# Decoding a codebook layer's weights one stage earlier: comparisons on GpSimd, three of four quarters inside the single-head attention

## The reference

```python
x = x + _L3_xattn_ref(_layernorm(x), ctx_4096, ...)   # cross-attention, 32 heads, 2048 keys
x = x + _L3_attn_ref(_layernorm(x), ...)              # one head of 128
x = x + _L3_ffn_ref(_layernorm(x), codebooks, bias, ln_weight, codes, centroids)

def _L3_ffn_ref(x2, ...):
    cw = _expand(centroids, codebooks)                # 32 x 512, looked up in 32 codebooks of 32 entries x 16
    dots = x2 @ cw.T
    dots = (dots - mean(dots)) * rsqrt(var(dots) + 1e-05) * ln_weight
    m = softmax(dots) > 0.5
    W = _expand(codes, codebooks)                     # 512 x 512, looked up in the same way
    y = x2 @ W.T + bias
    return y * (any(m, row)[:, None] & repeat(any(m, column), 16)[None, :])
```

## Time and profile before

| what | us |
|---|---|
| median of 3 runs | 1691.44 |
| the runs | 1689.5 to 1693.83 |
| the profiled execution | 1685.28 |
| its span, first to last instruction | 1683.5 |
| first TensorE instruction of L3a, of L3f | 1643.92, 1656.44 |
| GpSimd busy, of the span | 324.6 (19%) |
| TensorE busy, of the span | 1562.3 (93%) |

### The profile page before, as it was taken

How to read it: one execution, slowest core, us unless ns; L and a number is a source line. 1 busy time by engine, 2 the same in 40 slices (tenths; PEclk the granted TensorE clock), 3 DMA queues, 4 the chain that set the end, 5 groups by cost and what they waited for, 6 DMA issues and landing times. The chain is left out here.

```text
span 1683.5 us, 23015 instructions
## 1 busy us (share of the span) xinstructions
PE 1562.3 (93%) x7457; PEld 1167.1 (69%) x7457; DVE 1044.1 (62%) x2136; ACT 889.3 (53%) x1624; POOL 324.6 (19%) x280
## 2 busy tenths in 40 slices
PE   4999999999999988998989996997999999999986
PEld 4788778778775443487566664785777787777864
DVE  5666666675665882275478883664157667676663
ACT  4545554554554451264148884552266667666661
POOL 0000000000001340054136663450011011111110
PEclk9999999999999999999999998998999999999999
DMA  7011011011019107262362212536311122211012
GB/s 259 27 38 57 30 37 62 25 58 42 25 54 364 43 24 266 99 194 97 100 153 29 33 20 87 170 122 231 113 61 53 44 81 80 76 56 56 25 58 79
DMA packets 57282, 148.52 MB, mean 88 GB/s; under 512 B 5969, under 2 KB 28113, under 8 KB 48129
## 3 DMA queue, kind: packets, MB, share of 16 engines
q1 hardware_dynamic: 57216, 147.72, 26.8%
HBM read 133.55 MB, written 8.65 MB: 84 GB/s over the span
## 5 line engine op out<-in xcount | busy, mean ns | idle before, releaser
L1288 DVE TENSOR_TENSOR L3x_k_lo<-bank,L3x_k_hi 128x512 fp32r<-128x512 f32 x128 | 86.0, 687 | 52.2 <-ACT L3x_k_hi L1177 51.9
L2488 POOL TENSOR_TENSOR L2x_p_lo<-L2x_e_t,L2x_p_hi 128x512 fp32r<-128x512 f32 x80 | 105.3, 1326 | 63.0 <-ACT L2x_p_hi L2673 62.4
L664 DVE TENSOR_TENSOR L0x_k_lo<-bank,L0x_k_hi 128x512 fp32r<-128x512 f32 x128 | 85.7, 688 | 42.5 <-ACT L0x_k_hi L577 42.1
L376 PE MATMUL bank<-L0x_ctx_hi,L0x_w_hi 128*128 128x512 f32 x256 | 103.7, 405 | 4.2 <-DVE L0x_ctx_lo L603 4.2
L577 ACT ACTIVATE L0x_k_hi<-bank 128x512 fp32r<-128x512 f32 x128 | 74.2, 599 | 54.7 <-PE bank L482 54.7
L378 PE MATMUL bank<-L0x_ctx_hi,L0x_w_lo 128*128 128x512 f32 x256 | 101.0, 395 | 0.0
L886 POOL TENSOR_TENSOR L3x_v_lo<-L3x_v_raw,L3x_v_hi 128x512 fp32r<-128x512 f32 x32 | 40.5, 1302 | 310.2 <-ACT L3x_v_hi L1168 310.2
L377 PE MATMUL bank<-L0x_ctx_lo,L0x_w_hi 128*128 128x512 f32 x256 | 100.2, 391 | 0.0
L2716 DVE CUSTOM_DVE_ANT_0 L2x_junk<-bank,L2x_mask 128x512 f32<-128x512 f32 x128 | 85.1, 688 | 20.2 <-PE bank L2574 10.8
L1177 ACT ACTIVATE L3x_k_hi<-bank 128x512 fp32r<-128x512 f32 x128 | 74.1, 604 | 41.6 <-PE bank L1046 41.2
L336 POOL TENSOR_TENSOR L0x_r_hi<-L0x_r_sum,ones 128x4 fp32r<-128x4 f32 x8 | 1.6, 203 | 484.2 <-DVE L0x_r_sum L668 484.2
(11 more groups left out here) (630 smaller groups left out, 4388.3 us busy)
## 6 DMA issues: line engine op xcount, KB each, us to landing
L0x_w_kqv<-in_L0x_kqv SPq DMA_DIRECT2D x7, 1536.0 KB, 6.3
L0x_w_o<-in_L0x_o SPq DMA_DIRECT2D x8, 1024.0 KB, 4.8
L1a_w_o<-in_L1a_o SPq DMA_DIRECT2D x8, 1024.0 KB, 7.7
L2a_w_o<-in_L2a_o SPq DMA_DIRECT2D x8, 1024.0 KB, 7.2
L3x_w_q<-in_L3x_kq SPq DMA_DIRECT2D x8, 1024.0 KB, 5.4
L3x_w_o<-in_L3x_o SPq DMA_DIRECT2D x8, 1024.0 KB, 4.8
L3x_v_raw<-L3x_values SPq DMA_DIRECT2D x8, 1024.0 KB, 4.8
L0x_s<-in_ctx_t SPq DMA_DIRECT2D x4, 1024.0 KB, 12.1
```

The source lines that it names most:

```text
L376: pe.matmul(out, left[0], right[0], start=start, stop=False)
L664: dve.tensor_tensor(p_lo[:, kt % 4, :], ring_bank(kt)[:], bits(p_hi[:, kt % 4, :]), ALU.subtract).then_inc(p_ready, 1)
L1288: dve.tensor_tensor(p_lo[:, kt % 4, :], ring_bank(kt)[:], bits(p_hi[:, kt % 4, :]), ALU.subtract).then_inc(p_ready, 1)
L2488: pool.tensor_tensor(p_lo[:, t % 8, :], e_of(t), bits(p_hi[:, t % 8, :]), ALU.subtract).then_inc(low_pool, 1)
```

## The change

A class `CodebookWeights` holds the codes, the entries, the codebooks, `hot` and `w_t`, which now live through L3a and L3f (its tiles are called L3w in the rows). Its three transfers are issued in L3x behind L3a's. `mark` does the eight comparisons on GpSimd, after the last group of L3x and inside its block. `tensor(pe, t)` and `scalar(act, t)` are a quarter's four matmuls and two copies, now with one pair of banks (6 and 7), so that each quarter after the first waits for the copies of the one before. In L3a quarter 0 takes the place of the eight identity products, quarter 1 stands between `v` and the scores, and quarter 2 between the scores and the transpose. Quarter 3 takes the place of the identity products in L3f.

```diff
+class CodebookWeights:
+    def issue(self, sp):
+        sp.dma_start(self.codes[:], self.a["L3f_codes"]).then_inc(self.loaded, 16)
+        sp.dma_start(self.entry[:], self.a["L3f_entry"]).then_inc(self.loaded, 16)
+        sp.dma_start(self.books[:], self.a["L3f_books"]).then_inc(self.loaded, 16)
...
+    def mark(self, pool):
+        pool.wait_ge(self.loaded, 48)
+        for j in range(self.BG):
+            pool.tensor_scalar(self.hot[:, j, :], self.codes[:, j, :], self.entry[:], None,
+                               ALU.is_equal).then_inc(self.hot_ready, 1)
...
+    def tensor(self, pe, t):
+        pe.wait_ge(self.hot_ready, 2 * t + 2)
+        if t > 0:
+            pe.wait_ge(self.w_copied, t)
+        big, small = self.core.bank[6], self.core.bank[7]
...
+    def scalar(self, act, t):
+        act.wait_ge(self.w_ready, t + 1)
+        act.activation(self.w_t[:, t, 0:D], self.core.bank[6][:], ACT.Copy)
+        act.activation(self.w_t[:, t, D:], self.core.bank[7][:, 0:self.N], ACT.Copy).then_inc(self.w_copied, 1)
@@ L3x, GpSimd @@
                 with pool.Fori(1, NG) as g:
                     group(g)
+                core.codebook.mark(pool)
@@ L3a, TensorE @@
-                norm.keep_clock(pe)
+                codebook.tensor(pe, 0)
...
                 mm.then_inc(v_ready, 1)
+                codebook.tensor(pe, 1)
                 pe.wait_ge(qk_biased, 2)
...
+                codebook.tensor(pe, 2)
                 pe.wait_ge(p_ready, 1)
@@ L3a, ScalarE @@
                 norm.scalar(act)
+                codebook.scalar(act, 0)
+                codebook.scalar(act, 1)
...
+                codebook.scalar(act, 2)
@@ L3f @@
-                norm.keep_clock(pe)
+                codebook.tensor(pe, 3)
                 norm.tensor(pe)
-                for t in range(CT):
...
-                pe.wait_ge(w_copied, CT)
-                pe.wait_ge(c_copied, CT)
+                pe.wait_ge(codebook.w_copied, CT)
...
-                for j in range(BG):
-                    dve.tensor_scalar(hot[:, j, :], codes_sb[:, j, :], entry_sb[:], None,
-                                      ALU.is_equal).then_inc(hot_ready, 1)
```

More of the change, by code:

```diff
@@ L95, in __init__ @@
         self.values = None
+        self.codebook = None
         self.stale = []
@@ L1948, in _, with __init__, place_result, single_head_attention @@
                 dve.tensor_tensor(core.x[:], core.x[:], core.bank[0][:], ALU.add)
-def single_head_attention(core, name, wqkv, wo, qk_cols, rows):
+class CodebookWeights:
+    N = 32
+    BG = 8
+    def __init__(self, core, a):
+        self.core, self.a = core, a
+        self.st = st = Stage(core, "L3w")
+        self.books = st.sb("books", [P, self.BG, P])
+        self.codes = st.sb("codes", [P, self.BG, D + self.N], I32)
+        self.entry = st.sb("entry", [P, 1])
+        self.hot = st.sb("hot", [P, self.BG, D + self.N])
+        self.loaded = st.sem("loaded")
+        self.hot_ready = st.sem("hot_ready")
+        self.w_ready = st.sem("w_ready")
+        self.w_copied = st.sem("w_copied")
+    def issue(self, sp):
+        sp.dma_start(self.codes[:], self.a["L3f_codes"]).then_inc(self.loaded, 16)
+        sp.dma_start(self.entry[:], self.a["L3f_entry"]).then_inc(self.loaded, 16)
+        sp.dma_start(self.books[:], self.a["L3f_books"]).then_inc(self.loaded, 16)
+    def place_result(self):
+        self.w_t = self.st.sb("w_t", [P, CT, D + self.N])
+    def mark(self, pool):
[8 more added lines that the diff above has]
+        big, small = self.core.bank[6], self.core.bank[7]
+        for j in range(2):
+            pe.matmul(big[:], self.books[:, 2 * t + j, :], self.hot[:, 2 * t + j, 0:D], start=(j == 0), stop=(j == 1))
+        for j in range(2):
+            mm = pe.matmul(small[:, 0:self.N], self.books[:, 2 * t + j, :], self.hot[:, 2 * t + j, D:],
+                           start=(j == 0), stop=(j == 1))
+        mm.then_inc(self.w_ready, 1)
+    def scalar(self, act, t):
+        act.wait_ge(self.w_ready, t + 1)
+        act.activation(self.w_t[:, t, 0:D], self.core.bank[6][:], ACT.Copy)
+        act.activation(self.w_t[:, t, D:], self.core.bank[7][:, 0:self.N], ACT.Copy).then_inc(self.w_copied, 1)
+def single_head_attention(core, name, wqkv, wo, qk_cols, rows, a):
     nc = core.nc
@@ L1971, in issue @@
             sp.dma_start(bias[:], rows.to_broadcast([P, HD + D])).then_inc(rows_in, 16)
+            codebook.issue(sp)
+        core.codebook = codebook = CodebookWeights(core, a)
         following = yield issue
         norm = LayerNorm(core, st, core.bank[0])
+        codebook.place_result()
         qk_t = st.sb("qk_t", [P, 2, P])
@@ L2059, in _, with codebook_ffn @@
                 dve.tensor_tensor(core.x[:], core.x[:], core.bank[5][:], ALU.add)
-def codebook_ffn(core, name, books, codes, entry, rows):
+def codebook_ffn(core, name, rows):
     nc = core.nc
-    N = 32
-    BG = 8
+    codebook = core.codebook
+    N = codebook.N
     with Stage(core, name) as st:
-        books_sb = st.sb("books", [P, BG, P])
-        codes_sb = st.sb("codes", [P, BG, D + N], I32)
-        entry_sb = st.sb("entry", [P, 1])
         bias = st.sb("bias", [P, D + N])
@@ L2079, in issue @@
         def issue(sp):
-            sp.dma_start(books_sb[:], books).then_inc(loaded, 16)
-            sp.dma_start(codes_sb[:], codes).then_inc(loaded, 16)
-            sp.dma_start(entry_sb[:], entry).then_inc(loaded, 16)
             sp.dma_start(bias[:], rows.to_broadcast([P, D + N])).then_inc(loaded, 16)
         following = yield issue
-        norm = LayerNorm(core, st, core.bank[7])
-        hot = st.sb("hot", [P, BG, D + N])
-        w_t = st.sb("w_t", [P, CT, D + N])
+        norm = LayerNorm(core, st, core.bank[0])
+        w_t = codebook.w_t
         dots = st.sb("dots", [P, N])
@@ L2096, in codebook_ffn @@
         own = st.sem("own")
[L2097 to L2100, removed]
         dots_ready = st.sem("dots_ready")
@@ L2147, in _ @@
                 pe.wait_ge(taken_ready, 1)
-                pe.matmul(core.bank[6][:, 0:N], core.ones[:], taken[:], start=True, stop=True).then_inc(count_ready, 1)
+                pe.matmul(core.bank[3][:, 0:N], core.ones[:], taken[:], start=True, stop=True).then_inc(count_ready, 1)
             @block.scalar
@@ L2152, in _ @@
                 norm.scalar(act)
[L2153 to L2156, removed]
+                codebook.scalar(act, 3)
                 act.wait_ge(var_ready, 1)
@@ L2168, in _ @@
                 steps = Steps(dve, own)
-                dve.wait_ge(loaded, 64)
-                for j in range(BG):
-                    dve.tensor_scalar(hot[:, j, :], codes_sb[:, j, :], entry_sb[:], None,
-                                      ALU.is_equal).then_inc(hot_ready, 1)
+                dve.wait_ge(loaded, 16)
                 dve.wait_ge(dots_ready, 1)
@@ L2189, in _ @@
                 dve.wait_ge(count_ready, 1)
-                steps.then(dve.tensor_scalar(k_mask[:], core.bank[6][:, 0:N], 0.5, scal[:, 6:7], ALU.is_gt,
+                steps.then(dve.tensor_scalar(k_mask[:], core.bank[3][:, 0:N], 0.5, scal[:, 6:7], ALU.is_gt,
                                              ALU.mult))
@@ L2195, in _ @@
                 dve.tensor_tensor(core.x[:], core.x[:], y_sb[:], ALU.add)
+    core.end_with_last(codebook.st)
 def feature_cross_attention(core, name, a):
@@ L3269 @@
     "L3a": lambda core, name, a: single_head_attention(core, name, a["L3a_w"], a["L3a_o"], a["L3a_cols"],
-                                                       a["L3a_rows"]),
-    "L3f": lambda core, name, a: codebook_ffn(core, name, a["L3f_books"], a["L3f_codes"], a["L3f_entry"],
-                                              a["L3f_rows"]),
+                                                       a["L3a_rows"], a),
+    "L3f": lambda core, name, a: codebook_ffn(core, name, a["L3f_rows"]),
     "L3x": lambda core, name, a: normed_cross_attention(
```

## The result

| | before | after |
|---|---|---|
| median, us | 1690.47 (1689.17 to 1693.83, 6 runs) | 1678.79 (1674.34 to 1682.21, 6 runs) |
| ratio | | 0.9927, 95% interval 0.9909 to 0.9945 |
| profiled execution (span), us | 1685.28 (1683.5) | 1677.48 (1675.4) |
| from L3a's opening to the end of the span, us | 39.6 | 30.1 |

The kernel became faster, by 12.3 us worked out from the ratio (1690.47 x 0.0073; the interval makes that 9.3 to 15.4, and the two medians differ by 11.7). The forecast was 8.0 us less; 1678.79 us lies 0.7 us under the lower end of its range. The two profiled executions differ by only 7.8 us, and L3a opened in that of before at 1643.92, in that of after at 1645.30, 1.4 us later, for reasons ahead of the stages that the change touches. From L3a's opening on they differ by 9.5 us.

The account below looks back on a forecast made before the run. Bound by short engine-to-engine waits in the last stages: 3.2 us more in L3a, 0.5 and 12.37 less, 1.65 lost to half clock: 8.0 us less, median 1691.44 to 1683.4 us, range 1679.5 to 1690.5.

Parts of the forecast that it names:

- The comparisons on GpSimd: End of L3x: eight comparisons at 1.41 us each run 1627.7 to 1639.0, hidden, 4.6 us before L3x ends.
- the three estimates: Time of one 544-element GpSimd comparison, scaled from nearest rows: 0.57, 1.41 and 1.52 us.
- The room: GpSimd's idle time at the end of L3x: 15.9 us, so comparisons up to 1.98 us each cost nothing.
- VectorE beside GpSimd, the transfers: In L3x, GpSimd does not slow VectorE's 0.69 us subtractions, and the three transfers land in time: no cost.
- L3a, TensorE: +3.2: Moved quarters lengthen L3a by 3.2 us: 0.06 before the transposes, 2.18 before the scores, 0.96 before the transpose.
- case (a): Full clock stays through L3a and L3f; L3a's projection takes about 0.98 us; net -9.7 us, chance 0.22.
- L3f: 15.98 to 3.61: From L3f's opening to `dots`: 3.61 us instead of 15.98, 12.37 us less, at 2.4 GHz.
- The clock: Whether TensorE's clock falls to half around L3a's end and L3f's opening; three cases, net -9.7, -8.0 or -6.7 us.
- (b): Clock falls at about L3f's opening for 3.3 us, costing TensorE 1.65 us; net -8.0 us, chance 0.32.
- The rivals: GpSimd too slow, putting off L3a: 1701.3 us, chance 0.11; gain mostly given back: between -5 and +4, chance 0.13.

Follow-up runs that it names:

- marks_twice: The changed kernel with the eight GpSimd comparisons done twice, the quarters waiting for the second round; 1698.32 us in one run.
- before_filled: The kernel before with ten identity products in L3a's TensorE waits, decoding not moved; 1685.35 us, ratio 0.9979.
- before_again: The kernel before, unchanged, profiled and timed a second time; 1689.52 us, ratio 0.9999.
- the three repeats: Three further profiled runs of the unchanged kernel before; 1689.52, 1689.93 and 1690.75 us, each with a tail of 42.0 us.
- the second timing: The changed kernel, unchanged, timed again against the kernel before; 1677.94 us, ratio 0.9932.
- marks_filled: The kernel before with only the comparisons moved to GpSimd in L3x, plus ten identity products in L3a's waits; ratio 0.9966.

## Why the prediction was right in direction and short in size

- **The comparisons on GpSimd.** The size was off and the place held: 13.00 us for eight, 1.62 each from start to start, instead of 1.41, above the highest of the three estimates, so 2.8 us were spare instead of 4.6. (Of the nearest rows, called subtractions, the one of 2867 ns is a product; no bound changes by it.) The room was right: 1629.14 to 1644.98 is 15.84 us, against 15.9. marks_twice shows that beyond it each us counts in full. VectorE's took 0.84 us for two in the chain of before_filled, 0.42 each from start to start, so GpSimd's are nearly four times as long. The Trainium skill calls GpSimd's rate with one input roughly line-rate (GPSIMD Engine Reference, section 4.1), which the prediction read as about as fast as VectorE; these rows do not bear that out.
- **VectorE beside GpSimd, the transfers.** Right: 0.69 us, and no wait for a transfer in the tail.
- **L3a, TensorE: +3.2.** Right: the transposes 2.16 us after the opening (2.18), the scores 4.87 us after the projections instead of 2.84 (+2.03, forecast 2.18), the transpose 3.18 us after the scores (3.03). The output projection took 1.12 us instead of 1.46, where case (a) had put 0.98, and the stage is 15.34 us instead of 12.52.
- **L3f: 15.98 to 3.61.** Right for that pair of executions: 3.57 from TensorE's first instruction, which here comes 0.15 us behind the layer norm's. But "this is at 2.4 GHz" was true of the new side only. The 15.98 us held the half clock of before: with the full clock (before_filled) the same stretch is 1671.85 - 1657.71 = 14.14 us, and in before_again it is 1676.88 - 1659.26 = 17.62. The term is 10.6 to 14.1 us, by before's clock.
- **The clock. This step failed.** "I take (b), in the middle" charged the changed kernel 1.65 us, where two of its three profiles are case (a), with the clock at full. That is the smaller part. The larger is that the step asked only how long the clock of the changed kernel would be at half, and took before's 6.8 us as given; then "it lay 6.16 us under the median of the runs" was carried over as if it were noise that both kernels share. Of those 6.16 us, 2.4 were half clock that the three repeats had, and that this one execution escaped in the very stretch that the change rewrites. Case (a) with before's ordinary tail is 9.7 + 2.4 = 12.1 us, case (b) 10.4; measured were 12.3 and, in the second timing, 11.5.
- **The rivals.** Neither came true: nothing waits for GpSimd, and no gain was given back.
- **Luck.** The profiled execution was forecast at 1677.3 us and took 1677.48. Two misses cancel in this: its tail was 1.5 us shorter than forecast (9.5 us off instead of 8.0), and the stages ahead of it took 1.4 us longer.

What stays open: why the clock of before is at half for 6.8 us in one execution and for 13.7 in the others, with the same instructions in the same order. The traces show one difference: in the first profile it falls 10.7 us after L3a opens, in the output projection, and in the three others after 9.1 to 9.3 us, in the product with the values ahead of it. That product took 0.69 us in before_again, and in the first profile still

```profile
1653.09 0.49 PE L2025 MATMUL bank<-L3a_p_t,L3a_v 128*128 128x128 f32 x2 [0.38 <-DVE L3a_p_t L2055]
```

What makes it fall sooner or later, no run here shows.

## What to carry to other kernels

Where a string of short waits lies at the half clock, take several profiles before pricing it: the difference between a profile and the median of the runs can sit in the very stretch that is to be changed, and then it does not carry over. Work with no input from the path is worth moving into waits, but its gain is made of two parts, the time that it leaves on the path and the clock that it keeps up, and a run with mere filler in the same waits tells the second apart. Work that is put on an engine ahead of a common meeting point is free up to that point, and costs in full beyond it, with the clock on top if TensorE is idle meanwhile.

## What the runs showed of the hardware

- The same program had 6.8 us at half clock in one execution and 13.7 us in three others, across the same two stages; with ten identity products of 128x128 in L3a's waits the two profiles (before_filled, marks_filled) had the full clock there.
- A comparison of 128x544 int32 with a value for each partition took GpSimd 1.62 us from start to start, and VectorE 0.42; GpSimd's two-input subtraction of fp32 scaled to the same width is 1.41 us, from the earlier trace rows.
- Eight such comparisons beside VectorE's subtractions, which read PSUM and SBUF, did not slow these. That is the Trainium skill's rule (SBUF — State Buffer, Who interferes with whom), and the trace agrees: 0.69 us.
- After 11.3 us of waiting (marks_twice), TensorE worked on at half clock for the first part of L3a, and the stage took 4.1 us longer.
